# A router stage started early, its steps rolled into a loop, and 28 multiplications in a wait of the tensor engine

## What is computed

```python
x = _layernorm(x + _L0_attn_ref(x, ...))            # recurrent mixing, gates, cumulative sums
x = _layernorm(x + _L0_xattn_ref(x, ctx, ctx, ...)) # 16 heads against 1601 context rows
x = _layernorm(x + _L0_ffn_ref(x, ...))             # 8 experts, the 2 best for each token
```

```python
logits = einsum('bsd,de->bse', x, Wr) + br
_, top_idx = top_k(logits, 2)                 # weights: softmax over the two chosen
for e in range(8):
    h = relu(x @ W1[e] + b1[e])               # 256 -> 1024
    out = out + (h @ W2[e] + b2[e]) * w[:, :, e]
```

## Time and profile before

| what | value |
|---|---|
| median of 3 runs | 2202.6 us |
| the profiled execution, its own time | 2195.98 us |
| its span on the core | 2194.3 us |
| TensorE busy | 1981.7 us (90%) |
| VectorE busy | 1754.2 us (80%) |
| ScalarE busy | 1540.5 us (70%) |
| GpSimd busy | 736.3 us (34%) |
| granted TensorE clock, mean | 0.96 |
| data moved | 212.39 MB, 97 GB/s |

### The profile page before, as it was taken

The page is one execution under the profiler, slowest core; times in us unless marked ns, Lnnn a source line. Parts: engine busy times, 40 slices in busy tenths (PEclk is TensorE's granted clock), DMA queues, the critical chain, the costliest instruction groups (busy, mean ns, idle before and its releaser), DMA issues.

```text
span 2194.3 us, 43516 instructions
## 1 busy us (share of the span) xinstructions
PE 1981.7 (90%) x10630; PEld 1044.8 (48%) x10638; DVE 1754.2 (80%) x3559; ACT 1540.5 (70%) x4345; POOL 736.3 (34%) x983
## 2 busy tenths in 40 slices
PE   7898998899999999999999998888829999999994
PEld 3554555322322232222322221112729999999994
DVE  5889885799999999999999999998635555555554
ACT  4655565899999999999999999998402333233333
POOL 0112111244444444444444441111563333333333
PEclk9989999999999999999999999999859999999997
DMA  4111105776758576676668576661771222222225
GB/s 156 44 44 72 58 24 130 193 125 116 112 110 145 118 110 117 119 124 135 90 131 136 108 111 92 123 77 42 223 197 32 37 36 37 36 36 36 36 36 168
DMA packets 126117, 212.39 MB, mean 97 GB/s; under 512 B 31554, under 2 KB 94786, under 8 KB 124882
## 3 DMA queue, kind: packets, MB, share of 16 engines
q1 hardware_dynamic: 98272, 151.74, 37.8%
q0 software_dynamic: 26240, 59.00, 10.2%
q10 hardware_dynamic: 1554, 1.05, 0.2%
HBM read 138.38 MB, written 73.74 MB: 97 GB/s over the span
## 4 chain that ended last, share of the span: by engine, by line
PE 39%; ACT 30%; issue 18%; DVE 7%; POOL 3%; DMA 2%; ACTq 1%; DVEq 0%; SPq 0%; POOLq 0%
ACT w_all L1429 26%; PE psum L1715 12%; PE psum L1725 11%; PE psum L473 6%; DVE neg_max L1336 3%; POOL list_all L1595 3%; PE psum L1239 2%; PE psum L1271 2%; ACT w_all L822 1%; PE psum L1702 1%; DMA v_all<-w_all 1%; PE psum L500 1%; ACTq L1428 1%; DVE stats L1016 0%; DVE stats L1995 0%
## 5 line engine op out<-in xcount | busy, mean ns | idle before, releaser
L1429 ACT ACTIVATE w_all<-psum,neg_max 128x512 f32<-128x512 f32 (+1 forms) x1664 | 1111.1, 736 | 18.2 <-DVE neg_max L1336 16.6
L1336 DVE TENSOR_REDUCE neg_max<-psum 128x1 f32<-128x512 f32 (+1 forms) x1664 | 1024.9, 677 | 17.3 <-PE psum L1271 14.2
L1271 PE MATMUL psum<-qst,kst 96*128 96x512 bf16 (+1 forms) x1664 | 527.7, 389 | 73.1 <-ACT w_all L1429 63.1
L1239 PE MATMUL psum<-w_all 128*32 128x512 f32 (+1 forms) x3328 | 448.9, 612 | 9.5 <-DVE w_all L1350 9.3
L1271 PEld LDWEIGHTS psum<-qst,kst 96*128 96x128 bf16 (+1 forms) x1664 | 130.0, 98 | 658.1 <-ACT w_all L1429 639.0
L1769 ACT ACTIVATE hid<-psum,b 128x128 f32<-128x128 f32 x568 | 161.9, 368 | 393.1 <-PE psum L1715 393.1
L1429 ACT ACTIVATION_READ_ACCUMULATOR w_all<-psum,neg_max 128x1 f32 (+1 forms) x1664 | 426.8, 257 | 0.0
L1402 POOL TENSOR_TENSOR w_all<-vst,inv 128x64 f32<-128x64 f32 (+1 forms) x416 | 121.0, 291 | 658.3 <-DVE inv L1304 654.7
L1715 PE MATMUL psum<-xst,w 128*128 128x128 f32 x2272 | 267.4, 277 | 0.0
L1715 PEld LDWEIGHTS psum<-xst,w 128*128 128x128 f32 x2272 | 261.6, 193 | 0.1
L1725 PE MATMUL psum<-area,hid 128*128 128x256 f32 x1136 | 257.0, 380 | 0.0
(11 more groups left out here) (209 smaller groups left out, 1878.1 us busy)
## 6 DMA issues: line engine op xcount, KB each, us to landing
kst<-k_parts SPq DMA_DIRECT2D x384, 112.0 KB, 6.5
k_parts<-k_out POOLq DMA_DIRECT2D x52, 336.0 KB, 3.0
w_all<-in_W SPq DMA_DIRECT2D x16, 1024.0 KB, 11.9
area<-in_ctxT SPq DMA_DIRECT2D x16, 896.0 KB, 4.7
vst<-v_all SPq DMA_DIRECT2D x64, 224.0 KB, 9.2
qst<-q_parts SPq DMA_DIRECT2D x192, 64.0 KB, 5.9
v_all<-area POOLq DMA_DIRECT2D x13, 896.0 KB, 4.3
q_parts<-q_out POOLq DMA_DIRECT2D x24, 256.0 KB, 3.0
```

Of the source, the lines that this page charges most:

```text
L1239: last = pe.matmul(psum[j * PAD:(j + 1) * PAD, 6, :], v_scaled[0:r, pb, j, :], probs_at[pb][0:r, j, :], start=t == 0, stop=t == ST - 1)
L1271: pe.matmul(psum[0:r, 2 * sbuf + i, :], kst[:, h, j, t * P:t * P + r], qst[:, h, j, :], start=True, stop=True).then_inc(scores_ready, 1)
L1336: v.tensor_reduce(neg_max[0:r, sbuf, i:i + 1], psum[0:r, 2 * sbuf + i], AX_X, ALU.min) \
L1429: act.activation(probs_at[pb][0:r, j, :], psum[0:r, 2 * sbuf + i, :], ACT.Exp, bias=neg_max[0:r, sbuf, i:i + 1], scale=-1.0, accum_out=sum ...
```

## The change

Four things are done.

1. Batch 0's `project` moves on TensorE from behind the last `pv` to a place between the last-but-two and the last-but-one `pv` (two of them are still to come). On VectorE, batch 0's `norm_rows` moves to a place ahead of the copy of the last attention result.
2. The router's steps are no longer unrolled throughout: steps 0 and 1 stay written out, then a loop runs over pairs of steps (it has 2 turns on SP and TensorE, 3 on ScalarE and VectorE), and the rest is written out. Semaphore targets and some addresses in the loop come out of registers. The order of the work within a step is the same.
3. The semaphore for the experts' weights is split into one for `W1` and one for `W2`. For tile 0 VectorE copies the bias and `W1` before `name_rows`, and `W2` after `take_rows`; before, both copies stood between `name_rows` and `take_rows`.
4. Between the last `ranks` and the first `take`, TensorE multiplies a part of expert 0's `W1` by the identity 28 times (128 x 512 each, float32) into a PSUM bank that nothing reads then.

The diff at its core:

```diff
@@ attend_tensor, tile_step
                     if not is_over(tile, it):
                         scores(tile, 1, h, t, it)
+                    if tile == N_TILE + 1 and is_over(tile, it):
+                        pe.wait_ge(xwo_loaded, 16)
+                        pe.wait_ge(exp_done, 2 * N_SUB * it + 2 * LAST_OF_FIRST + 2 + 2 * CREDIT)
+                        project_rows(pe, 0, 0, 1, range(TT))
                     if tile >= LAG:
                         pv(tile - LAG, it)
@@ attend_vector, tile_step
+                    if tile == N_TILE + LAG - 1 and is_over(tile, it):
+                        v.wait_ge(v_scaled_ready, N_TILE * (it + 1))
+                        norm_rows(v, 0, 0)
@@ experts
+            def route_steps(eng, step, turns, last):
+                def one(c, it, h, like):
+                    step(c, it, h, like < B, 0 <= like - 1 < B, 0 <= like - 2 < B)
+                for c in range(2):
+                    one(c, 0, c, c)
+                with eng.Fori(1, turns) as it:
+                    for h in range(2):
+                        one(2 * it + h, it, h, 2 + h)
+                for c in range(2 * turns, last):
+                    one(c, c // 2, c % 2, c)
@@ experts_tensor
                 opened(pe, mm1_done, mm2_done)
-                pe.wait_ge(xwo_loaded, 16)
-                project(0, range(TT))
-                for c in range(B + 2):
-                    route_step(c)
+                route_steps(pe, route_step, B // 2 - 1, B + 2)
+                pe.wait_ge(w1_loaded, 16 * E)
+                for _ in range(SPINS):
+                    pe.matmul(psum[:, 5, :], ident[:], w1_all[:, 0, 0, 0:4 * P], start=True, stop=True)
                 pe.wait_ge(slots_ready, B)
                 take(0, 16)
@@ experts_vector
                 opened(v, y_scaled)
                 v.sem_inc(y_scaled, 1)
-                for d in range(3):
-                    name_rows(d, 16)
-                v.wait_ge(ffn_loaded, 32 * E)
-                at = copy_weights(slice(0, 1), 0)
-                v.wait_ge(xs_t_ready, 1)
-                take_rows(0)
-                v.wait_ge(b2_loaded, 16)
-                scale_bias(at, 0)
+                v.wait_ge(w1_loaded, 16 * E)
                 v.wait_ge(x2_ready, B)
                 for h in range(2):
                     v.wait_ge(x2_stored[h], 16 * B)
+                at = copy_first(slice(0, 1), 0)
+                for d in range(3):
+                    name_rows(d, 16)
+                v.wait_ge(xs_t_ready, 1)
+                take_rows(0)
+                v.wait_ge(w2_loaded, 16 * E)
+                copy_second(at, 0)
+                v.wait_ge(b2_loaded, 16)
+                scale_bias(at, 0)
                 tiles(v, tile_step)
```

More of the change, by code:

```diff
@@ L1135, in decoder_layer @@
             CREDIT = N_TILE
+            LAST_OF_FIRST = max(k for k in range(N_SUB) if score_buf[k] == 0)
             def free(k, buffer_of, it):
@@ L1540, in decoder_layer, with wide, project_rows @@
             assert TILES % DESTS == 3 and TT * D == HID and B >= 4
+            def wide(t):
+                return t.rearrange("p t d -> p (t d)").rearrange("p (n f) -> p n f", n=2)
+            def project_rows(pe, b, h, loads, ts):
+                if ts[0] == 0:
+                    wait(pe, y2_ready, b - 1)
+                    pe.wait_ge(route_loaded[h], 32 * loads)
+                for t in ts:
+                    at = psum[:, 2 * h + t // 2, (t % 2) * D:(t % 2 + 1) * D]
+                    for k in range(C):
+                        last = pe.matmul(at, at_in[:, h, k, t * P:(t + 1) * P], xwo[:, k, :], start=k == 0,
+                                         stop=k == C - 1)
+                if ts[-1] == TT - 1:
+                    last.then_inc(proj_ready, 1)
@@ new lines, in norm_rows @@
+            def norm_rows(v, c, h):
+                norms = Steps(NORM_STEPS * c)
+                wait(v, x2_ready, c)
+                v.wait_ge(proj_ready, c + 1)
+                v.tensor_tensor(wide(y2), psum[:, 2 * h:2 * h + 2], wide(x1_in[:, h]), ALU.add) \
+                    .then_inc(y2_ready, 1)
+                v.wait_ge(y2_ready, c + 1)
+                for t in range(TT):
+                    v.bn_stats(stats2[:, t], y2[:, t]).then_inc(dve_norm, 1)
+                    s = norms.next()
+                wait_alone(v, (dve_norm, s))
+                for t in range(TT):
+                    last = v.bn_aggr(moments2[:, t], stats2[:, t])
+                last.then_inc(moments2_ready, 1)
@@ L1684, in ranks, with route_step @@
                               start=True, stop=True).then_inc(ranks_ready, 1)
-                def route_step(c):
-                    if 0 <= c - 1 < B:
-                        turn(c - 1)
-                    if c + 1 < B:
-                        project(c + 1, (0, 1))
-                    if 0 <= c - 2 < B:
+                def route_step(c, it, h, norm, choose, place):
+                    more = not (isinstance(c, int) and c + 1 >= B)
+                    if choose:
+                        turn(c - 1, 1 - h)
+                    if more:
+                        project_rows(pe, c + 1, 1 - h, it + h + 1, (0, 1))
+                    if place:
                         ranks(c - 2)
-                    if 0 <= c - 1 < B:
+                    if choose:
                         route(c - 1)
-                    if c + 1 < B:
-                        project(c + 1, (2, 3))
+                    if more:
+                        project_rows(pe, c + 1, 1 - h, it + h + 1, (2, 3))
                 def take(half, count):
@@ L1738, in experts_scalar, with route_step @@
             def experts_scalar(act):
-                def route_step(c):
-                    h = c % 2
-                    if 0 <= c - 1 < B:
+                def route_step(c, it, h, norm, choose, place):
+                    if choose:
                         wait(act, logits_z_ready, c - 1)
```

126 lines of the change are left out of this document (48 added, 78 removed).

## The result

The kernel after takes 2211.05 us (median of 16 runs), the kernel before 2201.24 us (16 runs on the same chip): ratio 1.0043, interval 1.0034 to 1.0052. It is slower by some 9.5 us (7.5 to 11.4); +4.7 was forecast. One run of 7552.55 us, far out of line with all others, is left out of the ratio. The profiled execution took 2209.71 us, its span is 2208.0 us.

A forecast was written before the change was run, and what follows sets the result against it. GpSimd's block of 64 scatters, started by batch 0's `slots`, was taken to bound the kernel; +7.0 + 0.5 - 1.3 - 1.0 - 0.5 = +4.7 us on 2202.6 gave 2207.3, range 2199 to 2214.

The forecast's parts named there:

- C: Rival ahead of the first `take`: the 28 multiplications overrun at the low clock, +11 us, 2214; chance 0.05.
- D: Rival in the router's steps: half clock lasts over several, batches come late, +8 to +12 us, 2213; chance 0.12.
- only that moment moves it: GpSimd's block of 64 scatters, 82 us, moves only with the end of batch 0's `slots`, 1550.07.
- x2 of batch 0 is ready ... 2 us: After batch 0's early `project` and `norm_rows`, `x2` is ready at 1535.9 instead of 1537.9, the 2 us gain meant.
- The load issued 4.7 us later: On SP, the copy 4.7 us later delays the stores, `W1`'s last load and so the load of batch 2.
- so I shift the whole by 4.7 us: it lands at 1543.1: SP's load of batch 2, behind `W1` in the queue, lands at 1543.1 instead of 1538.4; TensorE waits some 6 us.
- The low clock behind the wait: TensorE's half `project` and `route` after the 6 us wait run at clock 0.50; `route` is done at 1550.2.
- S at +7, between +3.7 and +8.9: End of batch 0's `slots`: 3.7 us later at full clock, 8.9 at low clock; +7 taken.
- Loop +0.5: Loop entry and register instructions ahead of batch 0's `slots` on VectorE: 0 to 1 us, 0.5 taken.
- Copies -1.3: Weight copies no longer ahead of the first `take` result's copy: `take` of tile 1 starts 1.3 us sooner.
- Last landing -1.0: Landing of the last scatter, 6.26 us beside the experts' `W2` loads: up to 3.3 us can be won, 1 taken.
- The 28: Multiplications end 5 to 9 us before the first `take`, clock low again; 2.9 us gain at one in five: 0.5.

The follow-up runs named there:

- early_load: Kernel after, with SP's load of batch 2 issued ahead of the last attention stores; ratio to the kernel before 1.0013 (1.0003 to 1.0024).
- after_again: Kernel after, unchanged, measured again against the kernel before on chip B; ratio 1.0051 (1.0033 to 1.0068).
- copy_ahead: Kernel after, with the copy of the last attention result ahead of batch 0's `norm_rows` again on VectorE; ratio to the kernel before 1.0027 (1.0017 to 1.0037).
- best: Kernel after, with that copy ahead of `norm_rows`, the last `W1` load behind batch 3's load, and 42 multiplications; ratio to the kernel before 1.0043 (1.0028 to 1.0058).
- w1_late_only: Kernel after, with only the last expert's `W1` load moved behind the load of batch 3; ratio to the kernel before 1.0026 (1.0015 to 1.0036).
- both_loads_early: Kernel after, with batch 2's load ahead of the last attention stores and the last `W1` behind batch 3's load; ratio to the kernel before 1.0019 (1.0007 to 1.0032).
- late_project: Kernel after, with batch 0's `project` and `norm_rows` back at their old places; ratio to the kernel before 1.0009 (0.9999 to 1.0019).
- copies_only: Kernel before, with only the reordered weight copies and split semaphore added; ratio to the kernel before 0.9998 (0.9987 to 1.0008).
- late_spins_42: Kernel after, with batch 0's `project` and `norm_rows` back at their old places and 42 multiplications; ratio to the kernel before 1.0036 (1.0023 to 1.0049).

## Why the prediction was right, and where it was too small

The forecast, 2207.3 in 2199 to 2214, held the time, and the kind of slowdown is the one forecast: a late load, a wait, the low clock behind it. But +9.5 is twice +4.7, and 2211.05 lies above the forecast's own 2204.5 to 2210.5. It is inside the range because that reached to 2214 for cases C and D, which are not in this kernel; that part is luck. Its steps:

- **"only that moment moves it": right** for the chip of the result and B. The block kept its length (80.5 and 80.6 us before, 81.3 and 81.4 after), and the table follows S.
- **"x2 of batch 0 is ready ... 2 us" earlier: right, and shown alone** by `early_load`: logits 2.03 us earlier.
- **The load issued 4.7 us later: right in the profile (4.74), but by luck.** The copy was to come 4.7 us later, and without the chance drop it does (8.68 us after the last scores for 4.03). The load then comes only 3.35 us later (12.83 for 9.48). The prediction took the 1533.1 of the kernel before to be set by stores and `W1`; the stores had landed at 1530.13 + 1.67 = 1531.80, and what the load waited for was batch 0's L1808, which ends at 1531.82 + 1.22 = 1533.04: the load goes into the half that it reads. In the kernel after, L1584 has read it long before, and the load goes out when the stores have landed. The 1.3 us less were made up in the first profile by the chance drop.
- **"so I shift the whole by 4.7 us: it lands at 1543.1": the step that failed.** It landed at 1545.65, because it took 7.33 us from its issue (7.38 in `after_again`) where the shift kept the 4.8 of before: mis-sized by 2.6 us. Shifted as a whole, it would have had the old neighbours in the queue; it has others. `W1` had 2.99 us of a head start before and has 1.71 now. `W1` directly ahead: 7.41 us in `copy_ahead`, 4.49 in `best`, which differ at this place by that load alone. Stores and the next load directly behind, without `W1`: 6.02 in `w1_late_only`. Both: 7.33 to 7.57 in four profiles.
- **The low clock behind the wait: right in kind and in size up to the logits** (7.0 us from the start of `project` to the logits for 7.1 forecast; 3.6 before). From the logits to `slots` it was 9.7 and 9.5 us for 8.8 forecast. How long it lasts is not settled by the wait. Behind waits of 7.4 to 7.6 us, in four profiles, `route` took 3.42. Behind waits of 6.0, 3.8 and 0.9 us it took 1.85 to 1.87, though `project` ahead of it still took 3.4 to 3.7 there. But behind waits of 3.45, 3.79 (`early_load`) and 3.29 (`both_loads_early`) it took 3.56, and the clock stayed at 0.50 for 10 to 12 us. So the four microseconds of S for one of wait in `w1_late_only` hang on when the clock came back, and why it came back sooner there stays open. (The Trainium skill, TensorE: Matmul & The Clock Gate, part on the clock gate, has the throttled state as the default and full speed as something that activity earns. The low clock behind the waits agrees; in `early_load` it lasted for 12 us in which TensorE was busy throughout.)
- **S at +7, between +3.7 and +8.9: mis-sized.** Without the chance drop S is +10.6 on chip B, beyond the upper end, which was the case that occurred. From the last scores, 8.9 + 1.2 for the landing (1.4 earlier issued, 2.6 more to land) + 0.7 behind the logits is 10.8, for 10.9 in `after_again` against the first profile of before. With +10.6 in the place of +7 the sum would have been +8.3.
- **Loop +0.5:** not seen in S (36.6 unrolled for 36.9). Whether it is a part of the 3.3 us that `late_project` leaves isn't told by the runs.
- **Copies -1.3: right** (-1.6 after, -1.3 in `copies_only`).
- **Last landing -1.0: wrong.** It was 8.03 and 6.54 after, 6.26 and 8.03 before: no shift. The last of the experts' loads beside it had moved with the block: it landed at 1638.5 before and at 1653.3 after, within a microsecond of the last scatter both times.
- **The 28: right in effect,** clock low again, first tile 5.00 and 5.68 for 5.12 and 5.81. They were over 14.7 and 9.5 us ahead of the first `take`, for 5 to 9 forecast: the wait between the last `ranks` and the first `take` was 41.1 and 35.7 us, and it is 43.3 in the kernel before on chip B, for the 35.8 of the rows.

With the terms as measured: +10.6 - 1.3 = +9.3, for +9.5 measured and +11.2 on chip B. The intervals (7.5 to 11.4, 7.3 to 15.0) are wider than this agreement, so a further term of 2 us would not show.

Rivals: A fell with the 16 us at 0.50 (its terms give 0 to +2, not -1 to +2), B with the wait of 7.36 us, E with the slow first tile; a warm first tile is in `early_load`. C (overrun) is not in this kernel, but `late_spins_42` shows it with 42. D, a low clock over several steps that makes later batches late, fell for the kernel after, whose block has no gap; `both_loads_early` shows it.

What stays open: the 3.3 us of `late_project` and 5.2 of `late_spins_42`, what decides how soon the clock comes back, and why chips A and C need 20 us more. Their block takes 102.7 to 106.4 us for 80.5 to 84.6. A list of VectorE's waits in `late_project`, from 1553 to 1662 (us in total, times, longest), has at its head

```profile
DVE logits L1873 <- remote: 33.9, 3, 16.0
DVE slot_at L1841 <- remote: 7.8, 2, 4.5
```

and in the kernel before on chip B

```profile
DVE slot_at L1830 <- PE psum L1683: 7.2, 4, 2.5
DVE logits L1862 <- PE psum L1673: 2.4, 1, 2.4
```

"Remote" means that the profile knows no releaser. No kernel before was profiled on A or C, so that its 20 us have the same cause is only likely.

## What to carry to other kernels

A piece of work moved ahead on one engine pushes back what stood there, and here that was a copy on which, over four stores and a queue, the next batch's load hung; follow what is pushed back to its last reader before counting the gain. A load's landing time belongs to its neighbours in the queue, not to the load: after a move, list anew what is issued just ahead and just behind it. And price a wait of TensorE with the work behind it at half the clock, as a range: the clock was at 0.50 for 3 to 17 us in and behind the waits here, and behind two waits of 3.8 us a `route` took 1.85 and 3.56 us. Filling such a wait with idle multiplications pays only if they end just before the rows come (28 did in `early_load`, and 42 overran twice), which a fixed number can't do reliably when the wait is 27 to 43 us long by execution and chip.

## What the runs showed of the hardware that was not expected

- The same 512 KB half of a load landed 4.43 to 10.73 us after its issue (both in `both_loads_early`), by what stood ahead of it and behind it in the same queue.
- Behind a wait of 3.78 us the clock was back at 1.00 for `route` (1.85 us, `copy_ahead`), behind one of 3.79 us it stayed at 0.50 for 12 us of uninterrupted work (`early_load`).
- In 6 of 14 profiles the granted clock was 0.50 for 3 us right behind the last scores of the attention, with TensorE busy throughout, and cost 1.1 to 1.7 us. Two profiles of one kernel can differ by that and by up to 6.3 us in the moment at which the attention ends: compare stages from an anchor inside the trace.
- The last scatter landed after 6.26 and 8.03 us in two profiles of the same kernel, and after 4.58 to 8.82 over all.
- The kernel before takes 2201 us where the result was measured, 2200 on chip B and 2221 on A and C, and the ratios of changed kernels are still alike (1.0043 and 1.0051 there, 1.0039 and 1.0052 with one part left out here).
